# Four edits to a six-layer decoder kernel: input loaded and output stored by parts, one merged input stage, blocks returned by halves, and squares added on GpSimd ahead of one product with ones

## The reference

```python
q = causal_conv_silu(x @ Wq, conv_q_w, conv_q_b).reshape(b, t, H, K)
...
g = jax.nn.softplus(x @ Wfa @ Wfb + dt_bias).reshape(b, t, H, K)
beta = jax.nn.sigmoid(x @ Wb)
q = l2norm(q) * SCALE
k = l2norm(k)
o = kda_scan(q, k, v, g, beta)
gate = (x @ Wga @ Wgb).reshape(b, t, H, K)
var = jnp.mean(o * o, -1, keepdims=True)
o = o * lax.rsqrt(var + EPS) * o_norm_w * jax.nn.sigmoid(gate)
return o.reshape(b, t, D) @ Wo
```

## Time and profile before

| | us |
|---|---|
| median of 3 runs | 6057.47 |
| span of the profiled execution | 6055.8 |
| PE busy | 4922.0 (81%) |
| DVE busy | 3961.2 (65%) |
| ACT busy | 2819.8 (47%) |
| POOL busy | 2139.0 (35%) |
| start and end of the delta rule's first two parts | 1640 to 1744 |
| start and end of `delta_heads` | 1744 to about 4800 |

### The profile page before, as it was taken

How to read it: one execution, slowest core, us unless ns; L and a number is a source line. 1 busy time by engine, 2 the same in 40 slices (tenths; PEclk the granted TensorE clock), 3 DMA queues, 4 the chain that set the end, 5 groups by cost and what they waited for, 6 DMA issues and landing times. The chain is left out here.

```text
span 6055.8 us, 82551 instructions
## 1 busy us (share of the span) xinstructions
PE 4922.0 (81%) x24879; PEld 3229.1 (53%) x24965; DVE 3961.2 (65%) x6588; ACT 2819.8 (47%) x5024; POOL 2139.0 (35%) x2663
## 2 busy tenths in 40 slices
PE   5788747999577889988998899899898665888856
PEld 3556534566345666666666666666666432444423
DVE  4677664222337877877777777787777244888756
ACT  5555352111124555555555555555555213777632
POOL 2455400110215545445455454454454044000100
PEclk8899868999778999999999999999999787999989
DMA  2111005244331111111111111111110044111110
GB/s 61 29 29 29 15 28 194 73 144 157 122 99 50 37 48 42 43 55 50 43 40 49 55 47 44 49 40 41 52 46 28 11 136 140 54 54 54 42 57 28
DMA packets 355563, 365.99 MB, mean 60 GB/s; under 512 B 100193, under 2 KB 253281, under 8 KB 353921
## 3 DMA queue, kind: packets, MB, share of 16 engines
q1 hardware_dynamic: 335472, 286.73, 15.9%
q0 software_dynamic: 19744, 74.99, 3.5%
HBM read 264.76 MB, written 96.86 MB: 60 GB/s over the span
## 5 line engine op out<-in xcount | busy, mean ns | idle before, releaser
L1816 POOL TENSOR_TENSOR delta_rule_suffix<-delta_rule_suffix,delta_rule_prefix 128x256 f32<-128x256 f32 x448 | 513.6, 1146 | 1141.5 <-ACT delta_rule_prefix L1911 715.6
L2158 PE MATMUL delta_rule_proj<-delta_rule_hT,delta_rule_w_qkv 128*128 128x512 f32 x1024 | 466.4, 599 | 0.0
L2182 PEld LDWEIGHTS delta_rule_level<-delta_rule_qk_second,delta_rule_k_first 128*128 128x128 f32 x3072 | 392.9, 196 | 101.3 <-issue 86.6
L2182 PE MATMUL delta_rule_level<-delta_rule_qk_second,delta_rule_k_first 128*128 128x128 f32 x3072 | 425.6, 283 | 24.9 <-DVE delta_rule_L_large L1990 9.6
L481 DVE TENSOR_TENSOR_SCAN scan_hs<-scan_decay,scan_inp 128x512 f32<-128x512 f32 x256 | 308.6, 1216 | 194.4 <-PE scan_inp L543 90.9
L315 POOL TENSOR_TENSOR scan_hc<-scan_hs,scan_c_rows 128x512 f32<-128x512 f32 x256 | 334.6, 1312 | 282.1 <-DVE scan_hs L481 266.1
L2001 DVE TENSOR_TENSOR delta_rule_qk_second<-delta_rule_qk,delta_rule_prefix 128x512 f32<-128x512 f32 x448 | 363.0, 810 | 47.4 <-issue 12.1
L2059 DVE TENSOR_TENSOR delta_rule_prefix<-delta_rule_prefix 128x256 f32<-128x256 f32 x448 | 287.1, 641 | 160.2 <-PE delta_rule_level L2170 121.1
L1807 POOL TENSOR_TENSOR delta_rule_k_first<-delta_rule_qk,delta_rule_suffix 128x256 f32<-128x256 f32 x384 | 304.5, 793 | 196.3 <-PE delta_rule_level L2170 155.9
L2006 DVE SCALAR_TENSOR_TENSOR delta_rule_qk<-delta_rule_proj,delta_rule_conv_w,delta_rule_qk 128x511 f32<-128x511 f32 (+2 forms) x384 | 287.5, 749 | 103.7 <-ACT delta_rule_qk L1890 76.8
L2666 DVE TENSOR_REDUCE attend_top<-attend_scores 128x1 f32<-128x512 f32 x512 | 327.6, 682 | 42.3 <-DMA scan_c_rows<-bc_dram 42.3
(11 more groups left out here) (466 smaller groups left out, 11678.2 us busy)
## 6 DMA issues: line engine op xcount, KB each, us to landing
parts_dram<-qkv_parts POOLq DMA_DIRECT2D x64, 512.0 KB, 10.5
moe_w_d<-in_w_down SPq DMA_DIRECT2D x39, 512.0 KB, 4.3
scan_c_rows<-bc_dram SPq DMA_DIRECT2D x64, 256.0 KB, 3.7
delta_rule_w_qkv<-in_kda_wq SPq DMA_DIRECT2D x64, 256.0 KB
delta_rule_w_qkv<-in_kda_wk SPq DMA_DIRECT2D x64, 256.0 KB
delta_rule_w_qkv<-in_kda_wv SPq DMA_DIRECT2D x64, 256.0 KB
delta_rule_inv_beta<-beta_dram SPq DMA_DIRECT2D x64, 256.0 KB
delta_rule_w_o<-in_kda_wo SPq DMA_DIRECT2D x64, 256.0 KB, 4.7
```

The source lines that it names most:

```text
L1816: pool.tensor_tensor(first, first, whole_second, ALU.mult).then_inc(suffix_done, 1)
L2158: last = pe.matmul(to, w_qkv[p][:, i, k, :], hT[:, b % 2, k, :], start=(k == 0), stop=(k == DT - 1))
L2182: last = pe.matmul(level_ps[(i + 1) % 2][:, c, :], left, qk_second[:, i % 2, :, c * CHUNK // 2:(c + 1) * CHUNK // 2], start=True, stop=True)
```

## The change

1. The 4 MB load becomes four loads of 1 MB: the first in `load_constants`, without a wait, the others in the scan layer, after its parameters; DVE waits for each batch.
2. The store moves into the last layer: each row tile is stored by a 256 KB DMA when its sum is done.
3. `layer_norm` and `low_rank` of the delta rule become one stage, `delta_inputs`. The first batch is normalized and transposed after the statistics of its own four tiles. The beta products of the four batches go to four partition groups of one bank, with the weight padded to 32 columns, and the column form of beta comes from four transposes in place of 64 products. The loads of the weights begin with the stage. The last store of the gates comes after four stores of beta.
4. `return_blocks` stores the four blocks of the first unit, waits for them, loads `X[0]`, and then does the same for the second unit.
5. POOL adds `q_square` to `o_square` at slot 17, and PE does one product with ones at slot 19 in place of two at slot 13.

```diff
             def _(sp):
-                sp.dma_start(g["x"][:], g["x_dram"].rearrange("(t p) d -> p t d", p=P)).then_inc(x_loaded, 16)
-                sp.wait_ge(x_loaded, 16)
+                load_rows(sp, g, 0)
...
+                for b in range(1, B):
+                    load_rows(sp, g, b)
...
                     if j == 0:
+                        dve.wait_ge(g["x_loaded"][b], 16)
...
+                statistics(0)
+                invert(0)
+                for t in range(TPB):
+                    normalize(t)
+                statistics(1)
+                invert(1)
+                for b in range(1, B):
+                    for t in range(b * TPB, (b + 1) * TPB):
+                        normalize(t)
+                    if b > 1:
+                        copy_fg(b - 2)
+                copy_fg(B - 2)
+                dve.wait_ge(b_exp, 1)
+                dve.wait_ge(b_turned, 1)
+                dve.tensor_scalar(beta[:], beta[:], 1.0, None, ALU.add).then_inc(beta_done, 1)
...
+                copy_fg(B - 1)
...
+                        for b in range(B):
+                            last = pe.matmul(b_ps[b * PAD:(b + 1) * PAD, :], wb[:, k, :], hT[:, k, b * S:(b + 1) * S],
+                                             start=(k == 0), stop=(k == DT - 1))
...
+                for t in range(TPB):
+                    turn(t)
+                pe.wait_ge(w_loaded, 32)
+                for b in range(1, B):
+                    for t in range(b * TPB, (b + 1) * TPB):
+                        turn(t)
+                    low_rank(b - 1)
+                betas()
+                low_rank(B - 1)
+                pe.wait_ge(b_exp, 1)
+                for i in range(TPB):
+                    last = pe.transpose(col_ps[:, i, :], beta[:, i * P:(i + 1) * P], g["ident"][:])
...
-        SQUARE_SLOT, NORM_SLOT, LN_SLOT, EXP_SLOT, GATED_SLOT, OUT_SLOT, ADD_SLOT = 12, 13, 20, 20, 26, 23, 26
+        SQUARE_SLOT, SUM_SLOT, NORM_SLOT, LN_SLOT, EXP_SLOT, GATED_SLOT, OUT_SLOT, ADD_SLOT = 12, 17, 19, 20, 20, 26, 23, 26
...
                     for p in range(2):
                         for c, to in enumerate(diagonal(g["solved_dram"][p])):
-                            sp.dma_start(to, block_rows(solved, p, c)).then_inc(solved_stored, 16)
-                    sp.wait_ge(solved_stored, 16 * 2 * CHUNKS * (m + 1))
-                    for p in range(2):
+                            sp.dma_start(to, block_rows(solved, p, c)).then_inc(solved_stored[p], 16)
+                        sp.wait_ge(solved_stored[p], 16 * CHUNKS * (m + 1))
                         reach(sp, to_state, CHUNKS * (2 * m + p - 1))
                         sp.dma_start(flat(X[p]), square(g["solved_dram"][p])).then_inc(X_loaded[p], 16)
...
+                def back(slot, n):
+                    if slot == SUM_SLOT:
+                        pool.wait_ge(o_squared, n + 1)
+                        pool.tensor_tensor(o_square[:], o_square[:], q_square[:, n % 4, :], ALU.add).then_inc(o_summed, 1)
...
                     elif slot == NORM_SLOT:
-                        pe.wait_ge(o_squared, n + 1)
+                        pe.wait_ge(o_summed, n + 1)
                         pe.wait_ge(state_done, (CHUNKS - 1) * (n + 1))
-                        pe.matmul(flat(seq_ps), g["ones"][:], q_square[:, n % 4, :], start=True, stop=False)
-                        pe.matmul(flat(seq_ps), g["ones"][:], o_square[:], start=False, stop=True).then_inc(o_norm_done, 1)
+                        pe.matmul(flat(seq_ps), g["ones"][:], o_square[:], start=True, stop=True).then_inc(o_norm_done, 1)
...
+                    for t in range(NT):
+                        sp.wait_ge(out_added, t + 2)
+                        sp.dma_start(g["out_dram"][t * P:(t + 1) * P, :], g["x"][:, t, :]).then_inc(x_stored, 16)
```

More of the change, by code:

```diff
@@ new lines, in _, with statistics, invert, normalize @@
+                sp.wait_ge(stored, 16 * 3 * B)
+            @block.gpsimd
+            def _(pool):
+                pool.memset(wb[:], 0.0).then_inc(wb_zeroed, 1)
+            @block.vector
+            def _(dve):
+                def statistics(i):
+                    lo, hi = GROUPS[i]
+                    for t in range(lo, hi):
+                        dve.bn_stats(stats[:, t, :], g["x"][:, t, :])
+                    dve.drain()
+                    for t in range(lo, hi):
+                        dve.bn_aggr(mean_var[:, t, :], stats[:, t, :])
+                    dve.drain()
+                    dve.tensor_scalar(rstd[:, lo:hi], mean_var[:, lo:hi, 1], LN_EPS, None, ALU.add).then_inc(var_ready, 1)
+                def invert(i):
+                    lo, hi = GROUPS[i]
+                    dve.wait_ge(std_ready, i + 1)
+                    dve.reciprocal(rstd[:, lo:hi], rstd[:, lo:hi])
+                    dve.drain()
+                def normalize(t):
+                    if t >= RING:
+                        dve.wait_ge(h_turned, t - RING + 1)
+                    dve.tensor_scalar(h[:, t % RING, :], g["x"][:, t, :], mean_var[:, t, 0:1], rstd[:, t:t + 1],
+                                      ALU.subtract, ALU.mult).then_inc(h_ready, 1)
+                def copy_fg(b):
+                    dve.wait_ge(fg_done, b + 1)
+                    dve.tensor_copy(fgT[:, 0, b * S:(b + 1) * S], f_ps[b % 2][:]).then_inc(fg_copied, 1)
+                    dve.tensor_copy(fgT[:, 1, b * S:(b + 1) * S], g_ps[b % 2][:]).then_inc(fg_copied, 1)
+                statistics(0)
[13 more added lines that the diff above has]
+                dve.tensor_scalar(beta[:], beta[:], 1.0, None, ALU.add).then_inc(beta_done, 1)
+                dve.wait_ge(a_exp, 1)
+                dve.tensor_scalar(neg_a[:], neg_a[:], -1.0, None, ALU.mult)
+                copy_fg(B - 1)
@@ new lines, in _, with root, copy_hT @@
+            @block.scalar
+            def _(act):
+                def root(i):
+                    lo, hi = GROUPS[i]
+                    act.wait_ge(var_ready, i + 1)
+                    act.activation(rstd[:, lo:hi], rstd[:, lo:hi], ACT.Sqrt).then_inc(std_ready, 1)
+                def copy_hT(t):
+                    act.wait_ge(h_turned, t + 1)
+                    act.activation(hT[:, :, t * P:(t + 1) * P], turned[t % 2][:], ACT.Copy).then_inc(hT_copied, 1)
+                root(0)
+                for t in range(TPB):
+                    copy_hT(t)
+                root(1)
+                for t in range(TPB, NT):
+                    copy_hT(t)
+                act.wait_ge(a_loaded, 16)
+                act.activation(neg_a[:], neg_a[:], ACT.Exp).then_inc(a_exp, 1)
+                act.wait_ge(b_done, 1)
+                act.activation(beta[:], b_ps[:], ACT.Exp, scale=-1.0).then_inc(b_exp, 1)
+                act.wait_ge(b_turned, 1)
+                cols = root_beta[:].rearrange("p (c i) h -> p i c h", i=TPB)
+                act.activation(cols, col_ps[:].rearrange("p i (c h) -> p i c h", h=PAD)[:, :, :, 0:HEADS],
+                               ACT.Ln, bias=g["ones"][:, 0:1]).then_inc(col_ln, 1)
+                act.wait_ge(col_ln, 1)
+                act.activation(root_beta[:], root_beta[:], ACT.Exp, scale=-0.5)
@@ L1431, in _, with turn @@
             @block.tensor
             def _(pe):
-                pe.wait_ge(w_loaded, 48)
-                for c in range(B):
-                    if c >= 2:
-                        pe.wait_ge(copied, 2 * (c - 1))
-                        pe.wait_ge(beta_exp, c - 1)
-                    for w, to in ((wfa, f_ps), (wga, g_ps), (wb, b_ps)):
+                def turn(t):
+                    pe.wait_ge(h_ready, t + 1)
+                    if t >= 2:
+                        pe.wait_ge(hT_copied, t - 1)
+                    for k in range(DT):
+                        last = pe.transpose(turned[t % 2][:, k, :], h[:, t % RING, k * P:(k + 1) * P], g["ident"][:])
+                    last.then_inc(h_turned, 1)
@@ new lines, in betas @@
+                    last.then_inc(b_done, 1)
+                for t in range(TPB):
+                    turn(t)
[9 more added lines that the diff above has]
+                    last = pe.transpose(col_ps[:, i, :], beta[:, i * P:(i + 1) * P], g["ident"][:])
@@ L1475, in delta_heads @@
+                last.then_inc(b_turned, 1)
 def delta_heads(nc, g, neg_a, root_beta):
@@ L1560, in delta_heads @@
         blocks_solved = sc.sem("blocks_solved")
-        solved_stored = sc.sem("solved_stored")
+        solved_stored = [sc.sem(f"solved_stored{j}") for j in range(2)]
         X_loaded = [sc.sem(f"X_loaded{j}") for j in range(2)]
@@ L1849, in solve @@
                     pool.wait_ge(blocks_loaded, 16 * CHUNKS * 2 * (m + 1))
-                    reach(pool, solved_stored, 16 * CHUNKS * 2 * m)
+                    for p in range(2):
+                        reach(pool, solved_stored[p], 16 * CHUNKS * m)
                     pool.tensor_scalar(blocks[:, 0:SMALL, :], blocks[:, 0:SMALL, :], -1.0, None, ALU.mult)
@@ L3116, in program @@
```

(1 more changed line is left out.)

117 lines of the change are left out of this document (55 added, 62 removed).

## The result

The changed kernel takes 6074.27 us (median of 7 runs, 6066.99 to 6077.56) against 6053.86 us before, measured beside it: a ratio of 1.0034, 95% interval 1.0023 to 1.0045. So it is slower by 0.34%, which is inside the range and on the side that had the largest chance. The profiled execution has a span of 6073.1 us, 17.3 us above the one before; PE's busy time is 4879.9 us, DVE's 3986.0 us and POOL's 2212.8 us.

What follows compares the result with a forecast made beforehand. DVE was taken to bound slots 12 to 17 of a pass, PE the rest. 79.3 - 2.3 - 13.1 - 10.8 - 41 - 6 = +6.1 us on 6055.8 us gave 6064 us; 8 in 10 range 6022 to 6110 us.

Steps and rivals of the forecast that it cites:

- The removed products: Slot 13: 1.72 us of PE per pass goes, mostly becoming a wait; 0.09 us counted for an earlier L2091.
- The addition on POOL: Slot 17: an addition of 1.26 us puts `k_first` beside DVE's `prefix`, which ends 0.44 us later.
- the other reading: DVE's copy L2091 blocked beside POOL's addition, `prefix` and PE's product 0.14 us later, 8 us in all.
- The short passes: Short passes of `delta_heads` grow by 0.44 + 0.86 = 1.30 us, to 46.35 us; 61 passes by 79.3 us.
- The long passes: Passes with slot 12 at PE's lower clock: 28 at 1.2 us against 22 at 1.63 us, -2.3 us.
- rival C: In `delta_heads`, PE's new waits make the low clock the rule: all 61 passes long, 6103 us; chance 0.14.
- Start: The scan's statistics wait for parameters and 1 MB, not the 4 MB load; 13.1 us gained (10 to 14).
- Merged stage: Delta rule's inputs: column products go, beta products overlap, the meeting and weight load between parts go; 41 us gained.
- Rival D: In the merged stage the beta products run one after another: +9.8 us, 6074 us; chance 0.08.
- Halves: `X[0]` no longer waits for four of eight stores; 6 us gained (0 to 10).
- A: The two products at slot 13 were on PE's path and the late product finds a gap: 5934 us; chance 0.08.
- B: The addition on POOL costs nothing, DVE's `prefix` slipping in ahead: 6029 us; chance 0.15.

Runs made afterwards that it cites:

- sum_in_gap: The changed kernel with its one product with ones moved from slot 19 into PE's wait for `X` in slot 17, addition kept: 6003.9 us.
- one_at_19: The changed kernel without the addition on POOL: one product with ones, of `o_square` alone, at slot 19; 6039.6 us.
- one_at_13: Edits 1 to 4 without the addition, only the product of `o_square` left at slot 13; 5972.7 us.
- filler_two: The changed kernel with two more products with ones at slot 13, whose results are overwritten; 6072.0 us.
- longer: Edits 1 to 4 with both products at slot 13, one output-weight product of each pass repeated at slot 23; 6089.7 us.
- spare_sum: Edits 1 to 4 with both products at slot 13, plus a POOL addition at slot 17 that nobody reads; 5994.2 us.

## Why the prediction was nearly right

**What bounds a pass** held. Behind slot 17 every microsecond of PE is one of the pass: the product at slot 19 costs 0.85 us by sum_in_gap and 0.86 by one_at_19 (45.70 less 44.83), 0.86 predicted. PE idles 1.34 us ahead of level 1 (some 1.5 predicted), and DVE 0.84 us before its first addition to `X` behind slot 19 (0.85).

**The removed products** had a price after all, as long as there is no addition. I counted 0.09 us for an earlier `L2091`, since DVE had waited only 0.17 us for PE there; one_at_13 shows 0.21. The step that failed is "the product at 3247.64 waits for L1990 in any case, and DVE's work up to there hangs on POOL and on L2170": this is true of that product, but the two inverse steps between were late by as much as level 1 was, and the copy of `RT` hangs on them. In the changed kernel this price isn't drawn, as filler_two shows, and my 0.44 us didn't rest on it, since I let `prefix` end behind `k_first` too.

**The addition on POOL** was sized right, 1.27 for 1.26 us, and the collision fell where it was put, with `prefix` ending 0.27 us behind `k_first` (0.28 by the rows). The short pass came out between my two marks, 46.35 us with the collision and 45.8 without: the collision is there, at less than half its price. I had both of POOL's instructions begin 0.08 us behind the one before. That was the distance between `suffix` and the `k_first` that reads it. Between instructions that don't need each other it was -0.04 us by the rows of after (3085.87 + 1.23 = 3087.10, next start 3087.06; 3087.06 + 1.27 = 3088.33, next start 3088.29). So `k_first` came about 0.25 us earlier than I put it, and the net of addition and removed products is 0.40 - 0.21 = 0.19 us, not 0.44. This is the first term that was mis-sized. PE's wait for `X` shows the same: 71.2 us in 62 passes, 61.5 before, 0.16 us each. The copy from PSUM beside the addition was not blocked (0.69 us), so the trace agrees with the page of the Trainium skill named above, SBUF — State Buffer, section Who interferes with whom, and the 8 us of the other reading did not come.

**The short passes** thus grew by 1.04 us and not by 1.30. On 60 intervals that is 62 us in place of 78.

**The long passes** are the term that was mis-sized the other way. Taking the last 60 intervals, their sum is 2838.6 us after and 2755.6 before; less 60 short ones (46.08 and 45.04) that leaves 73.8 and 53.2 us for slow passes and for late loads. I had this fall by 2.3 us, with 28 slow passes; it rose by 20.6 us, with 46. This is most of rival C, which named 33 slow passes as its point, with 46 of 60 and not all. Its mechanism, that PE's new waits bring the low clock, is not the one shown: longer has no new wait and more slow passes. The two errors, -16 on the short passes and +23 on the long ones, nearly cancel, and that is luck.

**Start:** 11.2 us, 13.1 predicted (its own terms, 15.58 less 1.93 and 0.44, give 13.2). The statistics stand behind a DVE instruction that needs the parameter `d_skip`; its small load was issued at 3.64 us, while the first 1 MB was under way, and DVE waited 5.44 us for it. I had asked only what the statistics need. **End:** 10.85 us, 10.8 predicted. **Merged stage:** 43.1 us, 41 predicted. Rival D is refuted; the line view by form, in the window 1625 to 1690 us of after, shows the beta products with 32 columns side by side:

```profile
L1550 PE MATMUL kda_in_b<-kda_in_hT,kda_in_wb 128*32 128x512 f32 x32 | 3.6, 595 | 0.0
```

That is 3.6 us busy for 32 records, 4.0 predicted (four times the 1.06 us of the earlier trace rows would be 4.2). **Halves:** 7 us in the wait for `X`, 6 predicted. The changed kernel waits 18.3 us there, no less than the 16.9 before: with edit 5 alone, where PE comes earlier, the wait is 27.6 us, and I had put no cost on that.

Rivals A and B are refuted as wholes, but each held a part: A's 0.21 of 0.86 us where there is no addition, and B in spare_sum, where the addition misses `prefix`.

## What to carry to other kernels

Moving a product from a place where another engine's chain hides it to one where its own engine is the bound costs its full length, even when there are fewer of them; look for the wait of that engine first, as the one for `X` here, into which a product went at no cost. An addition on an idle engine isn't free if it pushes that engine's next instruction beside one of another engine that then takes twice its time. Two edits that act on the same wait have no price each of its own: the removal gave 0.21 us alone and nothing beside the addition. Where some passes run at the low clock, don't count their number as constant: here it went with the length of the pass, so try lengths.

## What the runs showed of the hardware that I had not expected

- The number of slow passes isn't a smooth function of the work: 25 to 29 of 60 in short passes of 44.83 to 45.23 us, 40 at 45.70, 52 at 45.91, 44 to 46 at 46.08, and once 31, each from one execution. A product of 0.86 us cost 1.4 us per pass in longer.
- An addition of 128x512 on POOL took 1.03 us with one tile as both inputs (spare_sum) and 1.27 us with two tiles (filler_two), both beside a DVE copy of `RT` that starts 0.84 or 0.85 us behind it; so the copy isn't the cause of the 0.24 us.
- DVE's `prefix` ended 0.27 or 0.28 us behind POOL's `k_first` however far into it it had started: 0.02 us (0.99 us long), 0.19 us (0.80, changed) and 0.40 us (0.61, filler_two).
- A small load issued 2.3 us ahead of a 1 MB one from the same queue (3.64 and 5.98 us), with the first 1 MB under way since 0.93 us, kept DVE waiting until 7.76 us.
